# Adding shifted products in 32x32 tiles of TensorE, in a dilated-attention kernel

## The reference, cut to what matters

```python
x = x + _L0_conv_ref(_gn(x), ...)   # block 1
x = x + _L1_conv_ref(_gn(x), ...)   # block 2

# block 1: q, k, v of 4 x 32 channels; for each dilation 1, 2, 4, 8 (2 heads each):
attn = softmax(einsum('bhdn,bhdkn->bhnk', qh, kp) * scale)   # kp: 9 shifted copies of k
out  = einsum('bhnk,bhdkn->bnhd', attn, vp)                  # vp: 9 shifted copies of v
# ... times a softmax gate per image and dilation
# block 2: p = W_qkv x + b; 4 heads; att = softmax(p p^T * scale); out = W_proj (att p) + b_proj
```

## Time and profile before

| | us |
|---|---|
| median of 3 runs | 83.57 (83.21 to 83.65) |
| the profiled execution | 83.74 |
| its span | 81.9 |
| PE busy | 69.4 (85%) |
| DVE busy | 67.5 (82%) |
| POOL busy | 41.5 (51%) |
| ACT busy | 29.3 (36%) |

### The profile page before, as it was taken

One profiled execution on the slowest core, in us unless ns is written; L12 is line 12 of the kernel. 1 busy time (PEld: TensorE's weight loads), 2 busy tenths in 40 slices (PEclk: granted clock), 3 DMA queues, 4 the chain that ended last, 5 costly groups with the idle time before them and its releaser, 6 DMA issues.

```text
span 81.9 us, 2442 instructions
## 1 busy us (share of the span) xinstructions
PE 69.4 (85%) x994; PEld 49.6 (60%) x994; DVE 67.5 (82%) x184; ACT 29.3 (36%) x92; POOL 41.5 (51%) x84
## 2 busy tenths in 40 slices
PE   4944999699995698999968797979999999999940
PEld 4933954367652466676857673667685778565520
DVE  2263879999999989999999699889999988678840
ACT  1753745973374000000030004220993281764200
POOL 7105008911940037999999999699990006000000
PEclk9998589999999999999999999999999999999999
DMA  1980064000000000000000000000000000011324
GB/s 14 317 293 16 0 164 102 1 0 0 8 0 4 0 12 0 0 0 4 8 0 0 0 0 0 8 0 0 0 0 0 8 0 12 0 64 64 132 97 163
DMA packets 2796, 3.06 MB, mean 37 GB/s; under 512 B 352, under 2 KB 2400, under 8 KB 2784
## 3 DMA queue, kind: packets, MB, share of 16 engines
q1 hardware_dynamic: 2496, 2.63, 10.5%
q10 hardware_dynamic: 288, 0.26, 0.9%
HBM read 1.84 MB, written 1.05 MB: 35 GB/s over the span
## 4 chain that ended last, share of the span: by engine, by line
DVE 36%; POOL 29%; PE 21%; ACT 4%; issue 4%; DMA 3%; DVEq 0%; POOLq 0%
PE ps L815 19%; DVE qk L602 15%; POOL acc L379 14%; POOL pv L379 12%; DVE pv L643 4%; DMA gx<-x_dram 3%; POOL rstd L342 3%; DVE acc L655 2%; DVE pv L655 2%; DVE x L674 2%; ACT xn L400 2%; PE ps L972 1%; ACT pT L436 1%; DVE x L706 1%; DVE prob L622 1%
## 5 line engine op out<-in xcount | busy, mean ns | idle before, releaser
L815 PE MATMUL ps<-prob,sel 64*128 64x192 f32 (+6 forms) x192 | 17.8, 313 | 2.7 <-DVE pv L643 1.6
L815 PE MATMUL ps<-xn,wp 128*32 128x256 f32 (+1 forms) x208 | 18.1, 410 | 1.9 <-DVE xn L574 1.1
L643 DVE TENSOR_TENSOR pv<-ps,v 128x128 f32<-128x128 f32 (+7 forms) x32 | 17.1, 567 | 1.8 <-PE ps L815 0.8
L815 PEld LDWEIGHTS ps<-prob,sel 64*128 64x128 f32 x192 | 13.7, 186 | 6.9 <-DVE pv L643 3.5
L379 POOL TENSOR_TENSOR pv<-pv 128x240 f32<-128x240 f32 (+3 forms) x24 | 14.1, 598 | 0.5 <-DVE pv L643 0.5
L815 PEld LDWEIGHTS ps<-xn,wp 128*32 128x32 f32 (+1 forms) x208 | 9.7, 122 | 6.9 <-issue 1.5
L342 POOL TENSOR_TENSOR rstd<-gvar,mhalf 128x2 f32<-128x2 f32 (+1 forms) x6 | 4.8, 808 | 16.2 <-DVE gvar L549 16.2
L379 POOL TENSOR_TENSOR acc<-acc,pv 128x256 f32<-128x256 f32 (+4 forms) x20 | 12.7, 638 | 0.5
L815 PE MATMUL ps<-idle 128*128 128x128 f32 x66 | 11.7, 320 | 1.1 <-DVE idle L533 1.1
L602 DVE TENSOR_TENSOR qk<-q,k 128x672 f32<-128x672 f32 (+7 forms) x21 | 11.4, 605 | 0.0
L815 PEld LDWEIGHTS ps<-idle 128*128 128x128 f32 x66 | 9.8, 220 | 2.4 <-DVE idle L533 1.0
(11 more groups left out here) (82 smaller groups left out, 91.4 us busy)
## 6 DMA issues: line engine op xcount, KB each, us to landing
out_dram<-x SPq DMA_DIRECT2D x8, 128.0 KB, 1.8
gx<-x_dram SPq DMA_DIRECT2D x2, 256.0 KB, 4.3
gx<-x_dram ACTq DMA_DIRECT2D x2, 128.0 KB, 3.1
sel<-selc_dram SPq DMA_DIRECT2D x4, 64.0 KB, 2.0
wp<-wpack_dram SPq DMA_DIRECT2D x1, 194.0 KB, 4.1
gx<-x_dram SPq DMA_DIRECT2D x1, 192.0 KB, 2.8
wp<-wpack_dram SPq DMA_DIRECT2D x1, 131.0 KB, 2.4
gx<-x_dram SPq DMA_DIRECT2D x1, 128.0 KB, 3.0
```

What stands on the lines that cost most here:

```text
L643: last = nc.vector.tensor_tensor(o, a, b, ALU.mult)
L815: return nc.tensor.matmul(o, w, m, start=start, stop=stop)
```

## The change

Unit (0,3) isn't added by POOL any more; PE adds it, slot by slot, in 32 x 32 tiles, and restores the other units of the first half in such tiles too. These products are put between the spreads of the second half: two images' worth ("near", banks 4 and 5) ahead of spread (1,0,0), the rest later. Units (1,2) and (1,3) are added by PE in the second sum; DVE only adds six pairs of border slots (`add_last`). POOL's rsqrts stand two adds later. project_second of group 1 and what follows it moves behind the sum, with new orders on DVE and ACT. There are 11 and 9 early dummies instead of 7 and 5; later ones go. The diff, cut:

```diff
-POOL_SUMS = (ND, 2)
-
-RSQRT_AFTER = ((1, 0, 4), (1, 1, 0))
+POOL_SUMS = (3, 2)
+
+RSQRT_AFTER = ((1, 0, 6), (1, 1, 2))
...
             for i in range(2):
                 copy_projection(0, i)
+            for i in range(2):
+                copy_pT(0, i)
+            squares(2)
             copy_projection(1, 0)
-            for i in range(2):
-                copy_pT(0, i)
+            squares(3)
+            attention_exp(0)
             copy_projection(1, 1)
             for i in range(2):
                 copy_pT(1, i)
-            attention_exp(0)
+            copy_fused(0, 1)
+            norm(2, 1)
             attention_exp(1)
-            squares(2)
-            squares(3)
-            copy_fused(0, 1)
-            copy_fused(1, 0)
-            norm(2, 1)
-            copy_fused(1, 1)
-            for g in range(2, 4):
-                for i in range(2):
-                    copy_projection(g, i)
+            for i in range(2):
+                copy_projection(2, i)
+            for i in range(2):
+                copy_fused(1, i)
+            for i in range(2):
+                copy_projection(3, i)
...
                 if ph and chunk == 0:
-                    dve.wait_ge(added, ADDS * (s + 1))
+                    if s < POOL_SUMS[0]:
+                        dve.wait_ge(added, ADDS * (s + 1))
+                    else:
+                        dve.wait_ge(restored, SLOTS)
...
-            def add_neighbours(ph, s):
...
-            def add_last_column():
-
-                s, middle = LAST_UNIT, 7
+            def add_last():
+
+                steps = ((2, 7, 6, 0), (3, 7, 6, 0), (2, 1, 0, 0), (2, 7, 8, 1), (3, 7, 8, 2), (2, 1, 2, 3))
                 dve.wait_ge(pv_ready, 12 * PHASES)
-                for n, ri in enumerate((0, 2)):
+                for s, onto, slot, after in steps:
+                    ci, ri = divmod(slot, 3)
                     r0, r1 = valid_rows(s, ri)
-                    c0, c1, _ = columns(DIL[s], 2)
-                    o, a = (pv[s][:, slot, :].rearrange("p (r c) -> p r c", c=W)[:, r0:r1, c0:c1] for slot in (middle, 6 + ri))
-                    if n:
-                        dve.wait_ge(last_added, n)
+                    c0, c1, _ = columns(DIL[s], ci)
+                    o, a = (pv[s][:, n, :].rearrange("p (r c) -> p r c", c=W)[:, r0:r1, c0:c1] for n in (onto, slot))
+                    if after:
+                        dve.wait_ge(last_added, after)
                     nc.vector.tensor_tensor(o, o, a, ALU.add).then_inc(last_added, 1)
...
-            for i in range(2):
+            multiply_pv(1, 2, 0)
+            second_norm_bias(0)
+            for i in range(1, 3):
                 multiply_pv(1, 2, i)
-            second_norm_bias(0)
             second_norm_bias(1)
-            multiply_pv(1, 2, 2)
-            multiply_pv(1, 3, 0)
-            add_neighbours(1, 2)
-            for i in range(1, 3):
+            for i in range(3):
                 multiply_pv(1, 3, i)
-            add_last_column()
-            attention_shift(0)
-            attention_shift(1)
-            attention_divide(0)
+            add_last()
             first_residual(2)
             first_residual(3)
+            attention_shift(0)
+            second_variance(2)
+            attention_divide(0)
+            second_variance(3)
             copy_fused(0, 0)
-            second_variance(2)
-            attention_divide(1)
-            second_variance(3)
             second_norm_bias(2)
             norm(2, 0)
+            attention_shift(1)
             second_norm_bias(3)
             for i in range(2):
                 norm(3, i)
+            attention_divide(1)
             copy_pT(2, 0)
...
-            def restore(g):
...
-            def sum_second():
...
+            def add_tile(ph, s, slot, js=range(SLOTS), start=False, stop=False):
+
+                if slot == 4:
+                    t, first, (r0, r1), (c0, c1) = acc, (ph * ND + s) * N, (0, H), (0, W)
+                else:
                     ci, ri = divmod(slot, 3)
-                    if slot == 7:
-                        pe.wait_ge(last_added, 2)
-                    tile(s, pv[s], slot * N, *valid_rows(s, ri), *columns(DIL[s], ci)[:2], stop=slot == 7)
+                    t, first, (r0, r1), (c0, c1) = pv[s], slot * N, valid_rows(s, ri), columns(DIL[s], ci)[:2]
+                dims = [[W, r1 - r0], [1, c1 - c0]]
+                at = r0 * W + c0
+                for j in js:
+                    rows = slice(32 * j, 32 * j + 32)
+                    last = mm(view(ps, 512 * (BANK[GROUPS // PHASES * ph] + j) + at, dims, 32 * s, 32), ident[rows, rows],
+                              view(t, first + at, dims, 32 * j, 32), start=start, stop=stop)
+                    if stop and s == LAST_UNIT:
+                        last.then_inc(restored, 1)
+
+            def add_slots(ph, s, slots, js=range(SLOTS), last=None):
+                for slot in slots:
+                    add_tile(ph, s, slot, js, start=slot == 4, stop=slot == last)
...
-            keep_clock(7)
+            keep_clock(11)
             first_stats(0)
-            keep_clock(5)
+            keep_clock(9)
             project(0)
...
             spread(0, 3, 2)
-            keep_clock(6)
-            for i in range(3):
+            near, far = range(2), range(2, SLOTS)
+            pe.wait_ge(qk_ready, ND * PHASES)
+            pe.wait_ge(id_loaded, 16)
+            pe.wait_ge(added, ADDS * 2)
+            for s in range(2):
+                add_slots(0, s, [4], near, 4)
+            pe.wait_ge(pv_ready, 11)
+            add_slots(0, 3, [4, 3, 5, 1, 0, 2], near)
+            keep_clock(4, 0)
+            for i in range(2):
                 spread(1, 0, i)
+            add_slots(0, 3, [4, 3, 5, 1], far)
+            spread(1, 0, 2)
+            add_slots(0, 3, [0, 2], far)
+            for s in range(2):
+                add_slots(0, s, [4], far, 4)
             spread(1, 1, 0)
-            restore(0)
+            pe.wait_ge(added, ADDS * 3)
+            add_slots(0, 2, [4], last=4)
+            add_slots(0, 3, [7, 6, 8], last=8)
             spread(1, 1, 1)
             group_stats(0)
-            restore(1)
             spread(1, 1, 2)
...
-            keep_clock(1, BANK[1] + 1)
             spread(1, 3, 0)
-            for i in range(2):
-                project_second(0, i)
+            project_second(0, 0)
+            spread(1, 3, 1)
+            project_second(0, 1)
+            spread(1, 3, 2)
+            for i in range(2):
+                transpose(0, i)
+            pe.wait_ge(pv_ready, 12 * PHASES)
+            pe.wait_ge(added, ADDS * sum(POOL_SUMS))
+            for s in range(2):
+                add_slots(1, s, [4], last=4)
+            add_slots(1, 2, [4, 3, 5])
+            add_slots(1, 3, [4, 3, 5, 1, 0, 2])
+            pe.wait_ge(last_added, 6)
+            add_slots(1, 2, [1, 7], last=7)
+            add_slots(1, 3, [7], last=7)
             for i in range(2):
                 project_second(1, i)
...
```

More of the change, by code:

```diff
@@ L219, in build @@
         added = sem("added")
-        dve_added = sem("dve_added")
         last_added = sem("last_added")
@@ L497, in _ @@
                 copy_projection(0, i)
-            copy_projection(1, 0)
             for i in range(2):
                 copy_pT(0, i)
+            squares(2)
+            copy_projection(1, 0)
+            squares(3)
+            attention_exp(0)
             copy_projection(1, 1)
@@ L929, in sum_second @@
-            def sum_second():
[L931 to L948, removed]
-                    ci, ri = divmod(slot, 3)
-                    if slot == 7:
-                        pe.wait_ge(last_added, 2)
-                    tile(s, pv[s], slot * N, *valid_rows(s, ri), *columns(DIL[s], ci)[:2], stop=slot == 7)
@@ L1062, in _ @@
             spread(1, 2, 2)
-            keep_clock(1, BANK[1] + 1)
             spread(1, 3, 0)
+            project_second(0, 0)
+            spread(1, 3, 1)
+            project_second(0, 1)
+            spread(1, 3, 2)
             for i in range(2):
-                project_second(0, i)
+                transpose(0, i)
[8 more added lines that the diff above has]
+            add_slots(1, 3, [7], last=7)
             for i in range(2):
                 project_second(1, i)
-            for i in range(2):
-                transpose(0, i)
-            for i in range(1, 3):
-                spread(1, 3, i)
+            attention(0)
+            group_stats(2)
             transpose(1, 0)
-            attention(0)
+            group_stats(3)
             transpose(1, 1)
-            attention(1)
-            sum_second()
             for i in range(2):
                 fuse(0, i)
-            pe.wait_ge(ashift_ready, 2)
-            keep_clock(2, BANK[1] + 1)
-            group_stats(2)
-            finish(0, 0)
-            keep_clock(2, BANK[1] + 1)
-            group_stats(3)
-            finish(0, 1)
-            keep_clock(1, BANK[1] + 1)
```

(16 more changed lines are left out.)

## The result

The changed kernel is slower: the ratio of its times to those of the kernel before is 1.017, 95% interval 1.011 to 1.024. Its four runs took 84.95, 85.14, 86.63 and 89.81 us beside a median of 83.39 before; the forecast was 84.6. Every ratio in this document leaves out the executions more than 1.5% above the fastest of their kernel (here the last two), many of which had the granted TensorE clock at half for 3 us or longer somewhere past the start. The profiled execution took 84.95, its span is 83.2.

A forecast was written before the change was run, and what follows sets the result against it. No engine was taken to bound it all, so the chain of waits was followed: 83.74 - 0.76 (early dummies) + 0.0 (sum) + 1.8 (tail) = 84.78, less 0.17 for the median: 84.6 us; range 82.4 to 85.8.

The forecast's parts named there:

- Early dummies, -0.76: Kernel start: more dummies fill TensorE's idle times, the clock stays at 2.4 GHz, DVE's first multiply comes earlier; -0.76 us.
- a rival at 0.04: Kernel start: the dummies come late, first statistics 0.65 us late and no gain, 86.0 us in all; chance 0.04.
- The early drop: Kernel start: granted TensorE clock at half (1.2 GHz) from about 7.5 to 10.8 us, expected to vanish.
- The walk to the second half: Second half's start: spread (1,0,0) 0.6 us late, (1,0,2) 1.5 late, DVE's first residual at 52.0 instead of 49.87.
- the near fill: TensorE products ahead of spread (1,0,0): longest chain 768 columns, 1.4 us, then four dummies, 1.07.
- the far fill: TensorE products ahead of spread (1,0,2): chain of 640 columns, 1.15 us, and two changes of tiling.
- A change: Switching TensorE between 64x128, 32x32 and 128x128 work: taken as 0.15 us each, bounds 0 and 0.2.
- DVE's last multiply, 62.2: End of DVE's second-half multiplies: 62.2 us, with the sum starting at 62.4 instead of 63.52, 1.1 won.
- the absent second restore gives 0.3 back: Second half: without the second restore 0.3 us returns, leaving DVE 1.85 late by multiply (1,2,0).
- The sum, 2.9: Second sum on TensorE: busy tiles hold later products, so 2.9 us instead of 1.91; residuals at 65.3, net 0.0.
- the rival at 1.85: Second sum: tiles independent, 1.85 us, -1.0 in the sum, 83.6 us in all; chance 0.22 together with a hidden tail.
- The tail, +1.8: From the residuals to the end: work moved behind the sum and its new order cost +1.8 us, bounds 0.9 and 2.2.

The follow-up runs named there:

- e1: The kernel before with 11 and 9 early dummies instead of 7 and 5, nothing else; 82.96 us, ratio 0.995.
- e3: The changed kernel with three dummies on TensorE in each of the two waits for ACT's squares (groups 0 and 1); 84.00 us, ratio 1.007.
- e6: e5 with the products of units (1,2) and (1,3) interleaved in the second sum; 82.42 us, ratio 0.989.
- e10: e6 with DVE's six adds reordered, slot 1 of unit (1,2) first, and TensorE waiting for each slot alone; 82.31 us, ratio 0.990.
- e7: e5 with ACT, DVE and TensorE behind the last multiply nearly in the old order; 84.36 us, ratio 1.011.
- e11: The kernel before with 7 and 9 early dummies, only the second group enlarged; ratio 0.996.
- e5: The changed kernel with the first half as before: POOL adds unit (0,3), 128-row restores, six dummies; 82.96 us, ratio 0.9925.

## Why the prediction was right in sum, and where its steps failed

**Early dummies, -0.76.** The mechanism was right and in the profiled execution the size too (-0.84). That was luck: on the mean it was -0.4. I had the other case, dummies at half clock that hold the statistics, as a rival at 0.04 with 0.65 of loss; e1's profile shows its half-way form (0.44 late), and seven of eleven profiles are like it. The early drop that I priced was, by the mean clock, in about a quarter of the executions before, and one profile couldn't tell. The choice between "gain" and "no gain" should have been a mean over when the clock rises.

**The walk to the second half.** Against the old positions less 0.84: spread (1,0,0) 0.66 late (forecast 0.6), spread (1,0,2) 1.29 (1.5), first residual 1.88 (2.1), POOL's wait ahead of rsqrt 1.60 (1.5), POOL's last add ending at 60.8 (61.7 less 0.8; but the terms listed for it, from 47.7, add up to 61.3, so the last is partly luck). The near fill's 768 columns took 1.45 to the dummies (forecast 1.4), and the far fill's 640 took 1.21 to the spread (1.15, and two changes of tiling). A change cost 0.1 rather than the 0.15 taken; I had read 0.1 in my own rows and then told of some 0.15. That spreads wait for the chain held as well: the far fill uses the rows of images 2 and 3 alone, and the spread, whose first product needs the other rows, starts only behind it, at 47.61. The Trainium skill, page TensorEngine Tiling (Array Packing), Key Properties, says that changing the tiling mode drains the engine, and the trace agrees.

**DVE's last multiply, 62.2.** Here a step failed. It came at 62.64 with 0.84 already won, so 1.3 late against the walk, and the sum started with no lead (62.71 is 63.52 less 0.81, all of it the early gain) where I had booked 1.1. I had put down "the absent second restore gives 0.3 back" and asked what was saved; I didn't ask what that restore did while TensorE had nothing else, though the same prediction told of the early clock drop in just such idle time. The half clock of 55.2 to 58.6 ate the lead: 1.0 on the two spreads of unit (1,2) alone. e3 shows it: with the clock held the kernel is 0.85 faster.

**The sum, 2.9.** Measured 2.80, and e6 confirms the reason, products held behind one whose tile is busy, against the rival at 1.85. The Trainium skill, page TensorE: Matmul & The Clock Gate, Part 3 (What overlaps and what doesn't), says that matmuls keep strict order in start and end. The trace agrees in the main, since products for free tiles started 0.70 after the first and not within 0.11. It isn't strict by the records: unit (1,3)'s four start at 63.41, ahead of the four `pv` ones at 63.55 (slot 5 of unit (1,2)), which were issued before them and waited for their own tiles. So they came at 0.70 and not at the 0.83 that I had. The interleaved order gave back 0.4 only, which I had put at 0.7 and then at DVE's door; e10 rejects the latter. What the rest is stays open.

**The tail, +1.8.** Measured +1.5. The arithmetic was fair, but I took the new order for a pure cost: the work moved behind the sum was counted as added there and, but for the times of the multiplies, not as removed ahead of it. e7 shows that with the old order the sum starts 3.0 later, so the order gains 1.4.

So 84.6 came out near partly by luck. In the profiled execution (84.95 beside 84.78 forecast) the sum started 1.1 later than forecast, through the clock that I hadn't seen falling. Against it stood terms too dear: the sum by 0.1, the tail by 0.3, and another 0.4 between DVE's last arithmetic and the end of the execution, which I had taken as unchanged.

## What to carry to other kernels

When a change takes work out of an engine's waiting time, ask what that work did for the clock: here a restore of 1.07 us kept TensorE at work between two waits, and without it 3.4 us ran at half clock. Filler must never reach past the moment at which the real work is ready, neither dummies nor chains on a single tile; a chain's length is the sum of its columns, however many tiles are idle beside it. In a tiled sum, issue products in an order in which each finds its tile free; and price moved work at both places, where it goes and where it came from.

## What the hardware showed that I hadn't expected

- 22 passes of dummies took 5.06 us or 4.09 us in different executions of the same opening; the moment at which the clock rises isn't fixed to the kernel's start. Dummies in front of waiting work then cost up to their whole length (nine took 3.70 in e11's profile, 2.25 in the changed kernel's).
- TensorE busy 1.33 of 3.0 us, with waits of 1.08 and 1.25 in it, was followed by half clock; busy 2.61 of 3.0 was not. In between it is not clear: busy 2.37 of 3.0 (65 to 68) was followed by half clock in e5's profile, and the same 2.37 (64 to 67) was not in e10's.
- In a sum over 32x32 tiles, products for free tiles started 0.70 us after the first, behind products whose tile was busy, and the reordered sum was 0.4 us shorter. They did pass the four products just ahead of them, which were waiting for their own tiles.
